# Keys and values from seven block products in four passes, stored once in float

## The chip, the cores and the metric

The kernel runs on one core of one Trainium2 chip. The metric is the device time of one execution in microseconds; three executions of the kernel before took 2989.80, 2990.52 and 2991.84 us, so the median is 2990.52 us.

## The reference, cut to what matters

Two layers follow each other on `x` (8 batches of 256 tokens, width 1024). The change touches only how the second layer gets its keys and values from the context, 2048 rows of width 1024, and how they reach its attention (32 query heads, 8 key heads, 128 wide). In short, for each batch:

```python
k = rope((ctx @ L1_xattn_wk).reshape(256, 8, 128))    # x * cos + concat(-x2, x1) * sin, over the token's angle
v = (ctx @ L1_xattn_wv).reshape(256, 8, 128)
p = softmax(where(mask, q @ k.T / sqrt(128), -1e9))    # query head h uses key head h // 4
x = x + tanh(g_xattn) * (concat_heads(p @ v) @ L1_xattn_wo)
```

All of it is in float32. The kernel gets that precision on TensorE by writing each factor as a high part (its value rounded to float32r) and a low part (what is left), and adding three products: high by high, high by low, low by high.

## The kernel before

The five engines (PE, ACT, DVE, POOL and SP, which issues DMAs) run one written-out program each, in order; they meet only in semaphores. `wait_ge(*at(name, key))` waits until the instruction that was marked with `inc(name, key)` is done. `three` (lines 147 to 152) issues the three products of one piece, each a matmul of 128 rows, a 128x128 stationary part and 512 columns. `weave` (from line 3130) sets the order in which the stages' programs follow each other on each engine; each stage is a generator and each `next` runs it to its next `yield`.

The stages are: keys and values (`kv_tensor`, `kv_scalar`, `kv_vector`, `kv_gpsimd`, `kv_sync`, 0 to 367 us), the first layer's attention by Fourier transforms (`ac_`, from 334 us), the first feed-forward layer (`f0_`), the queries (`qp_`, which already uses seven block products for eight with block sums on POOL), the attention with its output product (`at_`, about 1600 to 2800 us) beside which the last layer's weights are prepared (`wf_`), and the last layer (`f1_`).

Keys and values: 64 outputs of 128x512, each 8 pieces of 128 along the width (`C` = 8) by 3 matmuls. ACT rounds a loaded piece (`kv_high`), DVE or POOL subtracts to get the low part. The split weights stay in SBUF; the context is loaded and split in four blocks of 512 rows (`renew`). An output leaves its PSUM bank so: a value by a copy on ACT (high) and a subtraction on DVE (low); a key is first turned by its angles, by three products on DVE (lines 389 to 391), a sum on POOL (432), a copy on ACT (330) and a subtraction on POOL (434). High and low parts are stored in HBM, `kd[0]`, `kd[1]`, `vd[0]`, `vd[1]`. The last 8 value outputs are laid between the first steps of the `ac_` stage: its tables and its first 256 rows are loaded and split while PE still works on values.

Attention: 128 steps (`u`), four for each pair of a key head and 512 tokens (`n = u // 4`, 32 of them). `load_kv(n)` issues four DMAs for the high and low parts two steps ahead, and nothing else has to be done to them. Each step has on PE the transposes of weights, 12 score matmuls of 256 columns, 6 value matmuls and 24 output matmuls of 512; on DVE the maxima, the weights' scaling (`weigh`), the low parts and the sum into `at_xt`; on ACT the exponentials and copies; on POOL the low parts of the queries (`split_q`) and, in the first quarter, of the output weights (`split_wo`).

## Time and profile before

| | |
|---|---|
| median of three executions | 2990.52 us (2989.80 to 2991.84) |
| the profiled execution, first to last instruction | 2990.3 us |
| PE busy | 2959.3 us, 99% |
| DVE, POOL, ACT busy | 67%, 46%, 43% |
| bytes moved | 488.29 MB, mean 163 GB/s |

The profile gives for each engine the time in which it was busy, for each group of instructions their number, mean duration and the idle time in front of them with its releaser, and for each stretch of time the granted clock of TensorE (1.00 is 2.4 GHz). A matmul's duration is from its issue to its modelled end and overlaps its successor's, so the work rate of PE is read from the distance between starts and not from durations. Span and measured median differ by 0.2 us.

### The profile page before, as it was taken

The page shows a single profiled execution, that of the slowest core. Times are in us where ns is not written, and L with a number is a line of the kernel's source. Part 1 is how long each engine was busy: PE and PEld are TensorE (multiplying, and loading weights), DVE is VectorE, ACT ScalarE, POOL GpSimd, SP SyncE. Part 2 cuts the span into 40 slices and gives each one's busy share as a digit, 9 for nine tenths or more (in the row PEclk, how much of TensorE's full clock was granted, in tenths as well). Part 3 has the DMA queues.
Part 4 walks back from the last instruction along what each step waited for, and adds up shares of the span by engine and source line. Part 5 has one row for each costly group of instructions (what it writes and reads, how often), then busy time and mean ns, then how long its engine had stood idle before and what let it go on. Part 6 is the DMA issues. An engine that isn't in the chain of part 4 may idle for free.

```text
span 2990.3 us, 41114 instructions
## 1 busy us (share of the span) xinstructions
PE 2959.3 (99%) x14701; PEld 2482.3 (83%) x14701; DVE 2009.8 (67%) x4714; ACT 1282.8 (43%) x2686; POOL 1369.9 (46%) x1105
## 2 busy tenths in 40 slices
PE   9999999999999999999999999999999999999999
PEld 7888878887788878887888888888888888888887
DVE  4432478888655686679667777666776676666566
ACT  4111366665422422232223666555555545544332
POOL 2422388886422587777776334322322211111264
PEclk9999999999999999999999999999999999999999
DMA  7332421212555564455444787676677666665531
GB/s 254 127 120 99 166 70 50 78 64 75 191 177 166 197 179 113 113 149 152 109 112 120 242 268 239 227 242 209 193 221 244 189 196 204 208 194 166 225 108 76
DMA packets 320661, 488.29 MB, mean 163 GB/s; under 512 B 26236, under 2 KB 155644, under 8 KB 317644
## 3 DMA queue, kind: packets, MB, share of 16 engines
q1 hardware_dynamic: 319740, 484.23, 51.0%
q8 instruction: 118, 1.93, 0.3%
q10 hardware_dynamic: 720, 1.44, 0.1%
q14 instruction: 83, 0.68, 0.1%
HBM read 324.12 MB, written 161.48 MB: 162 GB/s over the span
## 4 chain that ended last, share of the span: by engine, by line
PE 61%; DVE 3%; DMA 0%; issue 0%; POOL 0%; ACT 0%; SPq 0%; DVEq 0%; ACTq 0%
PE PB L150 19%; PE PB L151 19%; PE PB L152 19%; PE PB L2401 4%; DVE qp_b L2150 1%; PE PB L2830 0%; DVE PB L2192 0%; DMA qp_raw<-in_wq 0%; DVE qp_r L2198 0%; DVE PB L2174 0%; DVE qp_c L2194 0%; DVE qp_r L2188 0%; DVE qp_r L2189 0%; POOL f1x L3046 0%; DMA qp_in<-xod 0%
## 5 line engine op out<-in xcount | busy, mean ns | idle before, releaser
L2567 POOL TENSOR_TENSOR at_ql<-at_qf,at_qh 128x512 fp32r<-128x512 f32 x128 | 166.2, 1299 | 833.9 <-ACT at_qh L2441 833.9
L2448 ACT ACTIVATE at_ss<-at_ss,at_sm,at_bs 128x256 f32<-128x256 f32 x512 | 301.9, 591 | 317.1 <-DVE at_sm L2528 317.1
L150 PE MATMUL PB<-at_woh,at_ah 128*128 128x512 f32 x1024 | 400.4, 391 | 0.6 <-DVE at_al L2550 0.6
L151 PE MATMUL PB<-at_wol,at_ah 128*128 128x512 f32 x1024 | 399.9, 390 | 0.0
L152 PE MATMUL PB<-at_woh,at_al 128*128 128x512 f32 x1024 | 399.5, 390 | 0.0
L2558 DVE SCALAR_TENSOR_TENSOR at_xt<-PB,gt,at_xt 128x512 f32<-128x512 f32 x256 | 192.1, 750 | 249.7 <-PE PB L152 249.5
L150 PE MATMUL PB<-qp_b,qp_a 128*128 128x512 f32 x896 | 350.2, 391 | 8.4 <-DVE qp_r L2196 3.8
L151 PE MATMUL PB<-qp_b,qp_a 128*128 128x512 f32 x896 | 349.3, 390 | 0.0
L152 PE MATMUL PB<-qp_b,qp_a 128*128 128x512 f32 x896 | 349.2, 390 | 0.0
L2220 POOL TENSOR_TENSOR qp_a<-qp_raw,qp_a 128x512 fp32r<-128x512 f32 x192 | 260.0, 1364 | 101.2 <-ACT qp_a L2112 98.5
L2112 ACT ACTIVATE qp_a<-qp_raw 128x512 fp32r<-128x512 f32 x192 | 113.5, 625 | 292.1 <-POOL qp_raw L2224 162.4
L2460 ACT ACTIVATE at_pth<-PB 128x512 fp32r<-128x512 f32 x256 | 139.2, 596 | 225.0 <-PE PB L2401 225.0
L152 PEld LDWEIGHTS PB<-at_woh,at_al 128*128 128x128 f32 x1024 | 192.3, 188 | 41.0
L150 PEld LDWEIGHTS PB<-at_woh,at_ah 128*128 128x128 f32 x1024 | 192.7, 188 | 37.5 <-ACT at_ah L2471 0.8
L151 PEld LDWEIGHTS PB<-at_wol,at_ah 128*128 128x128 f32 x1024 | 192.7, 188 | 35.3
L150 PEld LDWEIGHTS PB<-qp_b,qp_a 128*128 128x128 f32 x896 | 168.5, 188 | 45.9 <-DVE qp_r L2196 4.9
L152 PEld LDWEIGHTS PB<-qp_b,qp_a 128*128 128x128 f32 x896 | 168.6, 188 | 35.5
L151 PEld LDWEIGHTS PB<-qp_b,qp_a 128*128 128x128 f32 x896 | 168.6, 188 | 34.6
L2544 DVE TENSOR_TENSOR at_ptl<-PB,at_pth 128x512 fp32r<-128x512 f32 x256 | 164.8, 686 | 40.5 <-ACT at_pth L2460 40.5
L2524 DVE CUSTOM_DVE_ANT_0 at_ss<-PB,at_bi 128x256 f32<-128x256 f32 x512 | 185.4, 418 | 0.2
L150 PE MATMUL PB<-at_kh,at_qh 128*128 128x256 f32 x512 | 154.8, 302 | 0.0
L2538 DVE TENSOR_SCALAR at_ss<-at_ss,at_sm 128x256 f32<-128x256 f32 x512 | 149.3, 356 | 4.5
(314 smaller groups left out, 7570.6 us busy)
## 6 DMA issues: line engine op xcount, KB each, us to landing
at_woh<-wod SPq DMA_DIRECT2D x48, 1024.0 KB, 7.4
at_wol<-wod SPq DMA_DIRECT2D x48, 1024.0 KB, 9.6
qp_raw<-in_wq SPq DMA_DIRECT2D x32, 1024.0 KB, 5.4
qd<-qp_r SPq DMA_DIRECT2D x256, 128.0 KB, 2.5
at_qf<-qd SPq DMA_DIRECT2D x128, 256.0 KB, 3.4
at_rawo<-in_wo SPq DMA_DIRECT2D x32, 512.0 KB, 5.3
...
```

Source lines behind the costliest of these rows:

```text
L150: pe.matmul(o, ah, bh, start=start, stop=False)
L151: pe.matmul(o, ah, bl, start=False, stop=False)
L152: return pe.matmul(o, al, bh, start=False, stop=stop)
L2220: pool.tensor_tensor(qp_part(pair, i, 1), qp_weight(pair, i), asf(qp_part(pair, i, 0)), ALU.subtract).then_inc(*inc("qp_pool", ("w", pair, ...
L2401: m = pe.transpose(PB[1][:, 512 * k + P * c:512 * k + P * c + P], at_ss[s][:, c, P * k:P * k + P], idt[:, :])
L2448: m = act.activation(at_ss[s][:, c, :], at_ss[s][:, c, :], ACT.Exp, bias=z[:, 4 + c:5 + c], scale=at_bs[:, qn % 2, 8 + 2 * b + c % 2:9 + 2 ...
L2460: self.act.activation(at_pth[:, k, :], BK[2 + k], ACT.Copy).then_inc(*inc("at_act", ("pt", u, k)))
L2524: dve.tensor_tensor_reduce(out=at_ss[s][:, c, :], in0=PB[0][:, L * c:L * c + L], in1=at_bi[qn % 2][:, 2 * b + c % 2, :], scale=1.0, scalar ...
L2538: dve.tensor_scalar(at_ss[s][:, c, :], at_ss[s][:, c, :], z[:, 12 + c:13 + c], None, ALU.mult).then_inc(*inc("at_dve", ("weight", u, c)))
L2544: self.dve.tensor_tensor(at_ptl[:, k, :], BK[2 + k], asf(at_pth[:, k, :]), ALU.subtract).then_inc(*inc("at_dve", ("pt", u, k)))
L2558: self.dve.scalar_tensor_tensor(out=xt, in0=BK[6 + p % 2], scalar=gt[:, 2:3], in1=xt, op0=ALU.mult, op1=ALU.add).then_inc(*inc("at_dve", ( ...
L2567: self.pool.tensor_tensor(at_ql[n % 3][:, :], at_qf[n % 2][:, :], asf(at_qh[n % 3][:, :]), ALU.subtract).then_inc(*inc("at_pool", ("q", n)))
```

## The change

Context and weights are each cut in two by two blocks of 512x512 for a pass; a pass gives 1024 token rows by 1024 columns of keys or of values (`KV_PASSES`: values, keys, keys, values), from seven block products instead of eight, with four block sums on each side and sums of products behind. A product is 4 tiles (output 128x512) by 4 pieces (`c`) by 3 matmuls. Sums S1, S2 and S4 of the context's side are made on POOL, S3 and all sums T1 to T4 of the weights' side on DVE. Every product's 8 factor pieces are rounded on ACT and their low parts made on DVE (side `b`, and piece 3 of side `a`) or POOL (pieces 0 to 2 of side `a`); nothing of them is kept for the next pass. They go through a ring of 10 pieces a side, made 6 pieces ahead in each engine's program. The first three products run piece by piece across the four tiles, the others tile by tile.

Products are added up in SBUF (`leave`): 2 of 7 are copied by ACT, the others added by DVE, with one more sum on POOL. Keys and values are stored once, as plain floats: 64 stores of 256 KB where there were 128. Loads are 8 MB a pass, four times, where context and weights were loaded once (16 MB).

The turn by the angles and the split of keys and values move into attention, once for each `n`: on POOL two products (`turn_k`), and two low parts (`split_k`, `split_v`); on DVE two sums over 64 partitions (`join_k`); on ACT two copies. `load_kv` issues four DMAs as before: keys straight, keys with their halves swapped (two), and values.

The `ac_` stage's first loads wait for the last use of the raw blocks in whose place they go (`kv_spent`), several of its tiles move to other addresses, and its first steps are laid between the last products.

```diff
-        kd = [nc.dram_tensor(f"kd{i}", [G, P, T], F, kind="Internal").ap() for i in range(2)]
+        kd = nc.dram_tensor("kd", [G, P, T], F, kind="Internal").ap()
...
+        KV_SEQ = (0, 4, 3, 1, 6, 2, 5)
+        KV_PASSES = (("v", 0), ("k", 0), ("k", 1), ("v", 1))
+        KV_N = 7 * len(KV_PASSES)
+        KV_RING = 10
...
+        KV_FACTOR = {"a": ("a11", "a11", "a21", "s1", "a12", "a22", "a12"), "b": ("b11", "b11", "b12", "t1", "b21", "b21", "b22")}
+        KV_SUM = {("a", 3): ("kv_pool", "S1"), ("a", 1): ("kv_pool", "S2"), ("a", 2): ("kv_dve", "S3"), ("a", 6): ("kv_pool", "S4"),
+                  ("b", 3): ("kv_dve", "T1"), ("b", 1): ("kv_dve", "T2"), ("b", 2): ("kv_dve", "T3"), ("b", 5): ("kv_dve", "T4")}
...
+        def kv_low(side, c):
+            return "kv_dve" if side == "b" or c == 3 else "kv_pool"
+        def kv_bank(n, t):
+            return 4 + t % 2 if n >= KV_N - 2 else 4 * (n % 2) + t
+        def kv_emptied(n, t):
+            return ("kv_act" if n % 7 in (0, 2) else "kv_dve", ("out", n, t))
...
+        def kv_schedule(do):
+            do.begin()
+            for q in range(6):
+                do.prepare(q // 4, q % 4)
+            for n in range(KV_N):
+                do.product(n)
+                for t in range(4):
+                    if 4 * n + 6 + t < 4 * KV_N:
+                        do.prepare(n + 1 + (2 + t) // 4, (2 + t) % 4)
+                    do.tile(n, t)
+                    do.leave(n, t)
+                    do.load(n, t)
+                    if n >= KV_N - 2 and t % 2 and (n, t) != (KV_N - 1, 3):
+                        yield
+                if KV_N - 5 < n < KV_N - 2:
+                    yield
...
+            def chunk(self, n, t, c):
+                on, ts = self.on, slice(P * t, P * t + P)
+                for side in ("a", "b"):
+                    on.wait_ge(*at("kv_act", (side, n, c)))
+                    on.wait_ge(*at(kv_low(side, c), (side, n, c)))
+                rows, cols = ("a", "b") if KV_PASSES[n // 7][0] == "v" else ("b", "a")
+                m = three(self.pe, BK[kv_bank(n, t)], (kv_part(rows, n, c, 0)[:, ts], kv_part(rows, n, c, 1)[:, ts]),
+                          (kv_part(cols, n, c, 0), kv_part(cols, n, c, 1)), c == 0, c == 3)
+                if c == 3:
+                    m.then_inc(*inc("kv_pe", ("out", n, t)))
+                elif t == 3:
+                    m.then_inc(*inc("kv_pe", ("chunk", n, c)))
+            def product(self, n):
+                if n < 3:
+                    for c in range(4):
+                        for t in range(4):
+                            if c == 0:
+                                self.claim(n, t)
+                            self.chunk(n, t, c)
+            def tile(self, n, t):
+                if n > 2:
+                    self.claim(n, t)
+                    for c in range(4):
+                        self.chunk(n, t, c)
...
+        class KvScalar(Keys):
...
+            def prepare(self, n, c):
+                on, p, i = self.on, n // 7, KV_SEQ[n % 7]
+                for side in ("a", "b"):
+                    if (side, i) in KV_SUM:
+                        engine, what = KV_SUM[side, i]
+                        on.wait_ge(*at(engine, (what, p, c)))
+                        on.wait_ge(*at(*kv_loaded(KV_FACTOR[side][i], p, c)))
+                    if 4 * n + c >= KV_RING:
+                        on.wait_ge(*at(*kv_chunk_done(4 * n + c - KV_RING)))
+                    self.act.activation(kv_part(side, n, c, 0), kv_factor(side, n, c), ACT.Copy).then_inc(*inc("kv_act", (side, n, c)))
...
+        class KvVector(Keys):
...
+            def low(self, side, n, c):
+                self.on.wait_ge(*at("kv_act", (side, n, c)))
+                self.dve.tensor_tensor(kv_part(side, n, c, 1), kv_factor(side, n, c), asf(kv_part(side, n, c, 0)), ALU.subtract).then_inc(
+                    *inc("kv_dve", (side, n, c)))
+            def first_sums(self, p, c):
+                dve, on = self.dve, self.on
+                on.wait_ge(*at(*kv_loaded("b11", p, c)))
+                on.wait_ge(*at(*kv_loaded("b12", p, c)))
...
+                dve.tensor_tensor(kv_raw["t1"][:, c, :], kv_raw["b12"][:, c, :], kv_raw["b11"][:, c, :], ALU.subtract).then_inc(
+                    *inc("kv_dve", ("T1", p, c)))
+                on.wait_ge(*at(*kv_loaded("a11", p, c)))
+                on.wait_ge(*at("kv_pool", ("S1", p, c)))
+                dve.tensor_tensor(kv_raw["a21"][:, c, :], kv_raw["a11"][:, c, :], kv_raw["a21"][:, c, :], ALU.subtract).then_inc(
+                    *inc("kv_dve", ("S3", p, c)))
+            def prepare(self, n, c):
+                dve, on, p, k = self.dve, self.on, n // 7, n % 7
+                if n == 2:
+                    self.first_sums(0, c)
+                self.low("b", n, c)
+                if kv_low("a", c) == "kv_dve":
+                    self.low("a", n, c)
+                if k == 1 and p:
+                    self.first_sums(p, c)
+                b11, b12, b21, b22, t1 = (kv_raw[name][:, c, :] for name in ("b11", "b12", "b21", "b22", "t1"))
+                if k == 2:
+                    on.wait_ge(*at(*kv_loaded("b22", p, c)))
...
+                    dve.tensor_tensor(b11, b22, t1, ALU.subtract).then_inc(*inc("kv_dve", ("T2", p, c)))
+                if k == 3:
+                    dve.tensor_tensor(b12, b22, b12, ALU.subtract).then_inc(*inc("kv_dve", ("T3", p, c)))
+                if k == 4:
...
+                    dve.tensor_tensor(b21, b21, b11, ALU.subtract).then_inc(*inc("kv_dve", ("T4", p, c)))
+            def leave(self, n, t):
+                dve, on, p, k, bank = self.dve, self.on, n // 7, n % 7, BK[kv_bank(n, t)]
+                c11, u, f, st = (a[t][:, :] for a in (kv_c11, kv_u, kv_f, kv_st))
+                if k in (0, 2):
                     return
+                on.wait_ge(*at("kv_pe", ("out", n, t)))
+                if k == 1:
+                    on.wait_ge(*at("kv_act", ("out", n - 1, t)))
...
+                    m = dve.tensor_tensor(st, c11, bank, ALU.add)
+                if k == 3:
...
+                    m = dve.tensor_tensor(u, c11, bank, ALU.add)
+                if k == 4:
+                    on.wait_ge(*at("kv_pool", ("out", n - 1, t)))
...
+                    m = dve.tensor_tensor(st, f, bank, ALU.add)
+                if k == 5:
+                    dve.tensor_tensor(f, f, bank, ALU.add)
+                    m = dve.tensor_tensor(u, u, bank, ALU.add)
+                if k == 6:
+                    on.wait_ge(*at("kv_dve", ("out", n - 1, t)))
+                    m = dve.tensor_tensor(u, u, bank, ALU.add)
+                m.then_inc(*inc("kv_dve", ("out", n, t)))
...
+        class KvGpsimd(Keys):
...
+            def prepare(self, n, c):
+                pool, on, p, k = self.pool, self.on, n // 7, n % 7
+                if n == 2:
+                    self.first_sum(0, c)
+                if kv_low("a", c) == "kv_pool":
+                    on.wait_ge(*at("kv_act", ("a", n, c)))
+                    pool.tensor_tensor(kv_part("a", n, c, 1), kv_factor("a", n, c), asf(kv_part("a", n, c, 0)), ALU.subtract).then_inc(
+                        *inc("kv_pool", ("a", n, c)))
+                if k == 1 and p:
+                    self.first_sum(p, c)
+                a11, a12, s1 = (kv_raw[name][:, c, :] for name in ("a11", "a12", "s1"))
+                if k == 2:
...
+                    on.wait_ge(*at("kv_dve", ("S3", p, c)))
+                    on.wait_ge(*at("kv_pool", ("S1", p, c)))
+                    pool.tensor_tensor(a11, s1, a11, ALU.subtract).then_inc(*inc("kv_pool", ("S2", p, c)))
+                if k == 3:
...
+                    pool.tensor_tensor(a12, a12, a11, ALU.subtract).then_inc(*inc("kv_pool", ("S4", p, c)))
+            def leave(self, n, t):
+                if n % 7 == 3:
+                    on = self.on
+                    on.wait_ge(*at("kv_dve", ("out", n, t)))
+                    on.wait_ge(*at("kv_act", ("out", n - 1, t)))
+                    self.pool.tensor_tensor(kv_f[t][:, :], kv_f[t][:, :], kv_u[t][:, :], ALU.add).then_inc(*inc("kv_pool", ("out", n, t)))
...
+        class KvSync(Keys):
...
+            def begin(self):
+                for c in range(4):
+                    self.fetch("b11", 0, c)
+                for c in range(4):
+                    self.fetch("a12", 0, c)
+                    self.fetch("b21", 0, c)
+                for c in range(4):
+                    self.fetch("b12", 0, c)
+                    self.fetch("a21", 0, c)
+                    self.fetch("a22", 0, c)
+                for c in range(4):
+                    self.fetch("b22", 0, c)
+                self.sp.dma_start(idt[:, :], ident).then_inc(*landed("ident_in", 0))
...
             next(kv)
             next(ac)
-            for beside in (2, 2, 1):
-                next(kv)
-                next(kv)
-                for _ in range(beside):
-                    next(ac)
+            next(kv)
+            next(ac)
+            next(ac)
+            next(kv)
+            next(ac)
+            next(ac)
+            next(kv)
+            next(kv)
+            next(ac)
             for _ in kv:
                 pass
             next(ac)
...
+                if u % 4 == 3 and n < NG:
+                    do.join_k(n)
+                    do.split_k(n)
...
+                if u % 4 == 2 and n < NG:
+                    do.turn_k(n)
...
+            def join_k(self, n):
+                dve, on, kr, ks = self.dve, self.on, at_kr[n % 2], at_ks[n % 2]
+                on.wait_ge(*at("at_pool", ("sine", n)))
+                dve.tensor_tensor(kr[0:64, :, :], kr[0:64, :, :], ks[0:64, :, :], ALU.subtract).then_inc(*inc("at_dve", ("turned", n, 0)))
+                dve.tensor_tensor(kr[64:P, :, :], kr[64:P, :, :], ks[64:P, :, :], ALU.add).then_inc(*inc("at_dve", ("turned", n, 1)))
...
+            def turn_k(self, n):
+                pool, on, kr, ks = self.pool, self.on, at_kr[n % 2], at_ks[n % 2]
+                c, s = (qp_rope[:, k, :, :].rearrange("p t n -> p (t n)").unsqueeze(1).to_broadcast([P, 2, L]) for k in range(2))
+                on.wait_ge(*at("qp_rope", 1))
+                on.wait_ge(*at(f"at_k{n % 2}", ("swapped", n, 1)))
+                pool.tensor_tensor(kr[:, :, :], kr[:, :, :], c, ALU.mult).then_inc(*inc("at_pool", ("cosine", n)))
+                pool.tensor_tensor(ks[:, :, :], ks[:, :, :], s, ALU.mult).then_inc(*inc("at_pool", ("sine", n)))
+            def split_k(self, n):
+                self.on.wait_ge(*at("at_act", ("k", n)))
+                self.pool.tensor_tensor(at_kl[n % 2][:, :], at_kr[n % 2][:, :, :].rearrange("p b n -> p (b n)"), asf(at_kh[n % 2][:, :]),
+                                        ALU.subtract).then_inc(*inc("at_pool", ("k", n)))
+            def split_v(self, n):
+                self.on.wait_ge(*at("at_act", ("v", n)))
+                self.pool.tensor_tensor(at_vl[n % 2][:, :, :], at_vr[n % 2][:, :, :], asf(at_vh[n % 2][:, :, :]), ALU.subtract).then_inc(
+                    *inc("at_pool", ("v", n)))
...
-                sp.dma_start(asf(at_kh[s][:, :]), kd[0][g][:, rows]).then_inc(*landed(f"at_k{s}", ("high", n)))
-                sp.dma_start(asf(at_kl[s][:, :]), kd[1][g][:, rows]).then_inc(*landed(f"at_k{s}", ("low", n)))
-                sp.dma_start(asf(at_vh[s][:, :, :]), vd[0][rows, cols].rearrange("(t p) d -> p t d", p=P)).then_inc(*landed(f"at_v{s}", ("high", n)))
-                sp.dma_start(asf(at_vl[s][:, :, :]), vd[1][rows, cols].rearrange("(t p) d -> p t d", p=P)).then_inc(*landed(f"at_v{s}", ("low", n)))
+                sp.dma_start(at_kr[s][:, :, :].rearrange("p b n -> p (b n)"), kd[g][:, rows]).then_inc(*landed(f"at_k{s}", ("straight", n)))
+                for k in range(2):
+                    sp.dma_start(at_ks[s][64 * k:64 * k + 64, :, :].rearrange("p b n -> p (b n)"), kd[g][64 - 64 * k:P - 64 * k, rows]).then_inc(
+                        *landed(f"at_k{s}", ("swapped", n, k)))
```

## Rows read from the trace of the kernel before

**Rows 1.** The page: busy time, share of the span and instructions of TensorE.
```profile
PE 2959.3 (99%) x14701; PEld 2482.3 (83%) x14701; DVE 2009.8 (67%) x4714; ACT 1282.8 (43%) x2686; POOL 1369.9 (46%) x1105
```

**Rows 2.** Busy time by stretch: us, each engine's busy us (instructions), granted clock, DMA share, GB/s.
```profile
7.00:312.00 305.00, 304.94 (x1344) 252.21 (x1345) 116.68 (x167) 71.22 (x118) 97.38 (x76) 1.00 0.42 146
1600.00:2800.00 1200.00, 1199.10 (x6529) 1033.62 (x6528) 846.22 (x2521) 637.11 (x1613) 323.28 (x228) 1.00 0.66 212
760.00:800.00 40.00, 35.14 (x167) 26.84 (x166) 28.82 (x72) 16.91 (x22) 20.67 (x25) 0.96 0.51 168
1340.00:1400.00 60.00, 54.03 (x229) 43.58 (x228) 57.96 (x68) 15.71 (x28) 47.12 (x32) 0.97 0.51 129
```

**Rows 3.** Waits of PE, 0 to 660 us: total us, times, longest.
```profile
PE PB L659 <- POOL ac_slw L1025: 1.4, 3, 0.6
PE PB L298 <- ACT kv_wvh L350: 1.3, 1, 1.3
```

**Rows 4.** PE in order of time, late in the stage: start us, duration us.
```profile
304.62 0.39 PE L150 MATMUL PB<-kv_ch,kv_wkh 128*128 128x512 f32 x1
...
311.88 0.39 PE L152 MATMUL PB<-kv_ch,kv_wkl 128*128 128x512 f32 x1
```

**Rows 5.** Groups of instructions, 7 to 312 us: busy us, mean ns, idle before.
```profile
L432 POOL TENSOR_TENSOR kv_t<-kv_t,kv_t 128x512 f32<-128x512 f32 x31 | 40.0, 1290 | 101.7 <-DVE kv_t L391 101.7
...
L389 DVE TENSOR_TENSOR kv_t<-PB,kv_rt 128x512 f32<-128x512 f32 x31 | 21.4, 691 | 75.7 <-PE PB L152 68.3 <-POOL kv_ol L434 7.4
...
L330 ACT ACTIVATE kv_oh<-PB 128x512 fp32r<-128x512 f32 x24 | 13.6, 596 | 36.8 <-PE PB L152 31.7 <-DMA vd<-kv_ol 4.9
...
L404 DVE TENSOR_TENSOR kv_wvl<-kv_rc,kv_wvh 128x512 fp32r<-128x512 f32 x16 | 13.2, 853 | 14.0 <-ACT kv_wvh L350 14.0
...
L404 DVE TENSOR_TENSOR kv_wkl<-kv_rc,kv_wkh 128x512 fp32r<-128x512 f32 x16 | 10.9, 693 | 8.3 <-ACT kv_wkh L350 8.2
```

**Rows 6.** DVE and POOL at once, both on SBUF operands, in order of time.
```profile
1384.59 1.65 DVE L2194 TENSOR_TENSOR qp_c<-qp_c,qp_rope 128x512 f32<-128x512 f32 x1
...
1385.77 1.62 POOL L2216 TENSOR_TENSOR qp_raw<-qp_raw 128x512 f32<-128x512 f32 x1
```

**Rows 7.** The first microseconds: ACT and PE by time, then two stretches as in rows 2.
```profile
5.73 0.63 ACT L346 ACTIVATE kv_ch<-kv_rc 128x512 fp32r<-128x512 f32 x1 [1.76 <-DMA kv_rc<-in_ctxT]
...
7.03 2.06 PE L298 MATMUL PB<-kv_wvh,kv_ch 128*128 128x512 f32 x8 [1.30 <-ACT kv_wvh L350]
...
4.00:10.00 6.00, 4.69 (x16) 2.70 (x14) 3.08 (x3) 3.08 (x6) 2.62 (x2) 1.00 0.94 323
50.00:60.00 10.00, 10.00 (x46) 8.29 (x45) 4.74 (x7) 2.40 (x4) 0.81 (x1) 1.00 1.01 356
```

**Rows 8.** The passage to the `ac_` stage in order of time: DVE, POOL, ACT, PE.
```profile
324.55 0.96 DVE L847 TENSOR_TENSOR ac_tl<-ac_tr,ac_th 128x768 fp32r<-128x768 f32 x1
...
328.13 0.21 DVE L859 BATCH_NORM_AGGREGATE ac_st<-ac_st 128x2 f32<-128x12 f32 x1
334.52 1.23 DVE L943 TENSOR_TENSOR ac_ql<-ac_xn,ac_qh 128x1024 fp32r<-128x1024 f32 x1 [6.18 <-ACT ac_qh L710]
...
336.86 2.95 DVE L847 TENSOR_TENSOR ac_tl<-ac_tr,ac_th 128x1024 fp32r<-128x1024 f32 x3
...
330.19 0.24 POOL L983 TENSOR_SCALAR ac_st<-ac_st 128x2 f32<-128x2 f32 x1
...
331.87 1.52 ACT L702 ACTIVATE ac_xn<-ac_xb,ac_st 128x512 f32<-128x512 f32 x2 [4.25 <-POOL ac_st L991]
...
336.58 0.39 PE L150 MATMUL PB<-ac_qh,ac_th 128*128 128x512 f32 x1
```

**Rows 9.** One attention step in order of time: DVE, then PE.
```profile
1910.95 0.75 DVE L2558 SCALAR_TENSOR_TENSOR at_xt<-PB,gt,at_xt 128x512 f32<-128x512 f32 x1 [1.13 <-PE PB L152]
...
1911.83 1.14 DVE L2538 TENSOR_SCALAR at_ss<-at_ss,at_sm 128x256 f32<-128x256 f32 x4
...
1914.84 1.04 PE L2401 MATMUL PB<-idt,at_ss 128*128 128x128 f32 x8
```

509 lines of the change are left out of this document (186 added, 323 removed).

## The prediction

> **What bounds the kernel now.** I read the page first: PE is busy for 2959.3 of 2990.3 us [rows 1], so only what PE does or waits for can move the end. Then the stretches: from 7 to 312 us, where keys and values are made, PE has 304.94 of 305 us of work at the full clock of 2.4 GHz, and DVE 117, POOL 97, ACT 71 us; in the attention PE has 1199.10 of 1200 [rows 2]. The waits of PE say the same: up to 660 us they are single microseconds [rows 3]. So this stage is bound by the number of its matmuls. Their rate is in the order of time: 33 starts, 304.62 to 311.88 us, are 32 distances, 0.2269 us each [rows 4].
>
> **What goes.** Before, 64 outputs x 8 pieces x 3 = 1536 matmuls; after, 28 products x 4 tiles x 4 pieces x 3 = 1344. They have the same shape, so 192 x 0.2269 = **43.6 us** leave PE. A product is 48 matmuls, 10.9 us; a tile 2.72 us; a pass 76.2 us.
> The Trainium skill ("TensorE: Matmul & The Clock Gate", section "Wait — 56ns, not 53.3ns?") gives 215.7 ns between starts at 512 columns; by that the part would be 41.4 us. The row of this kernel decides.
>
> **Side engines, pass for pass.** ACT: 56 roundings at 0.63 [rows 7] and 8 copies at 0.60 [rows 5], 40 us of 76: no bound. POOL: 21 low parts, 12 sums, 4 sums of products, 37 x 1.29 [rows 5] = 48 us. DVE: 28 + 7 low parts and 20 sums, 55 instructions with both inputs in SBUF at 0.69 (the weights' low parts while POOL is idle), and 24 sums with one input in PSUM at 0.69 [rows 5]: 54.5 us. All fit, if they don't disturb each other. They do: where DVE and POOL both work on SBUF, a DVE instruction of this size takes 1.65 and the POOL instruction beside it 1.62 [rows 6], against 0.69 and 1.29 alone. So a POOL instruction can cost DVE 1.65 - 0.69 = 0.96 us. The lower bound is the opening, where 16 low parts on DVE met 8 on POOL and took 853 ns for 693 [rows 5]: 16 x 0.16 / 8 = 0.32. Between them a pass is 54.5 + 37 x 0.32 = 66 us or 54.5 + 37 x 0.96 = 90 us of DVE, beside 76.2 of PE. I take 0.65, between them since here both engines are released by the same ACT copies, 0.63 apart, but DVE is not in demand all the time as in rows 6's stretch (57.96 of 60 us [rows 2]): 78.5 us, though back-to-back instructions overlap by some 0.05 each, which gives 75. It is just covered. The last piece of a product is made from 2.7 us into the product before, and needed 2 us into its own, some 8 us after it can be ready; this takes the bunched sums (positions 7, 1 and 2 of a pass) nearly. I put **3 us** (0 to 30) for waits in passes 2 to 4.
>
> **The start.** Before, the first matmuls can go with high parts alone, at 7.03 us [rows 7]; now a piece waits for all four parts, so for the POOL low part, 1.29 after the ACT copy that ends at 6.36: about 7.8, **0.8 us** later. Data: product 2 needs three blocks, so 7 blocks, 7.3 MB, by its last piece at 37.8 us, and the T2 sums (in DVE's order ahead of the next piece) the eighth. At 323 to 356 GB/s [rows 7] eight blocks are there by about 27 us: loads are hidden, unless the rate falls to the 146 GB/s of the stage [rows 2], where the supply followed demand. The engines are not hidden: for each of product 2's pieces, S1, T1, S3, two low parts, S2 and T2 go through DVE and POOL, about three POOL and four DVE instructions, 5.5 us at the crowded rate, from 20 us (when ACT has copied the first sums) to about 38; then low part and S4 on POOL, low part and T3 on DVE and a sum of products for each of product 3's, 3.2 us. Product 3 is the first by tiles: it wants all four pieces within 2 us of 40.5 us, and gets the last at about 47.9. So **5.4 us**. Bounds: 0.6 with 0.32 for a meeting, 11 if product 2 is late as well. Together 6.2.
>
> **The passage to `ac_`.** Before, 8 outputs (43.5 us) lie beside it, the first two ahead of the tables and statistics; the chain is table low part at 324.55, statistics to 328.34, POOL to 331.8, ACT to 334.5, the queries' low part to 335.75; PE takes it at 336.58 [rows 8]. So it has only 0.8 us of room and is 11.2 us long. Half of it waits for a context split on POOL (its statistics start at 330.19), which now comes earlier: 9.5 us remain. After the change DVE reaches it when product 25 is through, T + 11.9 if T is that product's start, and ends at T + 21.4. PE has only product 25 and half of product 26 before the spectra, 16.3 us, and 2.7 of spectra: it asks at T + 19.0, **2.4 us** early. Then DVE has three low parts and four sums of products (4.5 us) and the second table's low part, 1.2 [rows 8], ahead of the odd spectra: ready at T + 27.1, asked at T + 24.2, **2.9 us**. The correlation behind has 1.6 us of room. What DVE is late by in product 25 comes on top; I put 6.0 in all, 0.5 to 9.
>
> **The clock.** Where PE stood for 4.9 us in 40, and 6 in 60, the mean granted clock was 0.96 and 0.97 [rows 2]: part of the time at 1.2 GHz, 1.6 and 1.8 us lost. Two such places: **1.5 us**, 0 to 3.5.
>
> **Attention.** Per key head and block, 32 times: POOL 4 x 1.29, DVE 2 x 0.69, ACT 2 x 0.62: 165, 44 and 40 us beside 1200 in which POOL has 323, DVE 846 and ACT 637 [rows 2]. DVE's two sums come ahead of `weigh`, in a gap of 1.13 us (1909.82 to 1910.95); they push it by 0.25, and it ends at 1912.97, 1.87 before PE's transposes at 1914.84 [rows 9]. The keys' low part is ready at 1914.2 of such a step, the scores want it at 1915.6. The cover of both is that room; without it each is about 0.3 us x 32. On POOL the wait for the swapped keys has `split_wo` behind it, but the keys were issued seven microseconds before. The moved steps issue four DMAs on SP's queue as before; in the keys' stage SP has half the stores and twice the loads. The first `n` falls into the end of the queries' stage. I put **1 us**, 0 to 4; not below nothing, as no matmul goes there.
>
> **Sum.** 2990.3 - 43.6 + 6.2 + 3 + 6.0 + 1.5 + 1 = 2964.4, and 0.2 to the median: **2964.5**.
>
> **Rivals.**
> A. All of it is hidden: a meeting costs 0.32, so the start costs 1.4 us, the passes nothing, the passage 5: 2990.5 - 43.6 + 6.5 = 2953. For it: the opening's own rows. Against it: the 1.65 of rows 6. From 2948 to 2956.
> B. DVE becomes the stage's bound, and the kernel is slower. Its mechanism is the meeting of two-SBUF-input instructions on DVE with POOL at the full 0.96: 90 us a pass for 76.2, less the 0.05 of overlap for 79 instructions, 86: 10 us x 4 = 40 and, with start 11, passage 9 and clock 3.5, 2990.5 - 43.6 + 63 = 3010. It gives a loss from (43.6 - 17) / 4 = 6.7 us a pass on, so from about 0.87 us per POOL instruction. The clock of a starved PE would add to it. For it: both engines' programs bunch their sums; against it: POOL has no more than half of the time, and a DVE instruction with a PSUM input beside a POOL one took 0.69 [rows 5].
> The Trainium skill ("SBUF — State Buffer", section "Who interferes with whom") has the rule for this: a DVE instruction with two SBUF inputs and a POOL instruction that reads SBUF hold one port in turn, each whole. By it every meeting costs the full POOL instruction, which is B if they always meet. Rows 6 agree with the rule; how often they meet, no row shows.
> C. In between: DVE is late by 2 to 5 us in each pass: 2976 to 2985, by the same rows at 0.75 to 0.8.
> D. The attention is not free: the keys' low part comes late in every fourth step by 1 us, 32 us: 2990.5 - 43.6 + 16.7 + 32 = 2996. The gain would be nearly gone and the kernel slightly slower. For it: 1.4 us of room only; against it: it is POOL's first work in that step and POOL idles there.
> E. The matmuls don't get fewer on the clock, as the new operands' layout slows the stream. The queries' stage does the same products in the same layout, so 2 in 100.
>
> **How the numbers follow.** Forecast with its own range 2956 to 2976: 0.56. A: 0.10. C: 0.17. B: 0.09, of which 0.02 ends within 0.2% of before. D: 0.06, half of it within 0.2%. E: 0.02. The range 2949 to 2984 leaves out B, D and E and the tail of A and C, about 2 in 10. A measurement of this kernel tells 0.2%, 6 us, from no change (2984.5 to 2996.5): faster 0.83, within 0.07, slower 0.10.
>
> **What would show it.** In the changed kernel: 1344 matmuls in the stage and the first `ac_` matmul some 27 us earlier than 333.86; PE waits of about 5 us between 40 and 50 us whose releasers are DVE or POOL low parts; two waits of 2 to 3 us at the first spectra; DVE instructions with two SBUF inputs at a mean near 1.1 us in the stage, near 0.8 for A, near 1.4 for B; DVE busy over 90% of passes 2 to 4; no new waits of PE in attention but a few tenths. The prediction is wrong if the steady passes starve PE, if the 8 MB of the start come slower than 300 GB/s, or if a load at a pass boundary is late, which I take as covered by the ten microseconds between a block's last use and its next.

## The result and the profile after

The changed kernel takes 3031.94 us (median; 3026.1 to 3042.75), the kernel before 2990.66 (2989.8 to 2991.84) beside it: a ratio of 1.014, 95% interval 1.0121 to 1.016. It is some 41 us slower, where 26 us faster was forecast. The profiled execution spans 3030.8 us, against 2990.3.

The page, busy time by engine; it answers to [rows 1]:

```profile
PE 2944.2 (97%) x14509; PEld 2460.7 (81%) x14509; DVE 2268.2 (75%) x4916; ACT 1379.4 (46%) x2878; POOL 1676.8 (55%) x1303
```

The 192 matmuls are gone (14701 - 14509), and yet PE is busy for only 15 us less: slower matmuls count as busy. To see where the time went I read in each trace when PE first takes certain tiles, in us from the start of the span:

```
kernel            ac_qh    at_kh    f1w     span    at_kh to f1w
before            336.6   1617.0   2818.6   2990.3   1201.6
after             331.0   1612.2   2859.1   3030.8   1246.9
e1_straight       328.2   1607.7   2809.1   2980.9   1201.4
e2_turn_last      328.1   1609.4   2845.9   3017.9   1236.5
e12_weigh_only    328.0   1611.3   2841.2   3013.3   1229.9
e9_weigh_early    328.2   1611.5   2820.5   2992.3   1209.0
e6_weigh_act      328.1   1609.5   2876.7   3048.5   1267.2
e7_both           329.9   1608.1   2875.4   3047.4   1267.3
e4_fill           369.3   1659.6   2912.6   3084.7   1253.0
e4b_fill_r        329.7   1611.8   2863.9   3035.8   1252.1
e3_pool_small     301.3   1582.5   2834.9   3006.6   1252.4
e5_no_dve_sums    314.1   1594.8   2841.1   3012.9   1246.3
e10_start_dve     324.8   1609.5   2821.4   2993.5   1211.9
e11_more_dve      318.9   1602.6   2812.9   2984.7   1210.3
e13_two_chunks    318.9   1601.8   2813.2   2984.9   1211.4
e14_last_pass     319.9   1598.9   2809.2   2981.0   1210.3
e15_both_moves    318.4   1595.8   2804.9   2976.6   1209.1
```

`ac_qh` is the first work that needs the whole chain of the passage, so it marks the end of the stage of keys and values; `at_kh` begins attention, `f1w` is the last stage. The mark is not quite the end: in the trace of before 96 matmuls of keys and values lie behind it, after the change 72, so that only 168 of the 192 are gone by then, 38.1 us. From before to after: the stage gains 5.6 us, the middle loses 0.8 although the other 24 lie there, attention loses 45.3, the last stage nothing: 40.5 us in all. The same code reached `ac_qh` between 328.0 and 331.0 us in seven profiles, so differences there count from 3 us on.

Stretches of the changed kernel, as in [rows 2] (us; each engine's busy time and instructions; granted clock; DMA share; GB/s):

```profile
0.00:60.00 60.00, 46.34 (x160) 34.02 (x161) 49.17 (x41) 29.81 (x54) 44.49 (x32) 0.86 0.50 172
45.00:65.00 20.00, 13.86 (x35) 9.86 (x35) 20.00 (x21) 9.55 (x18) 14.56 (x10) 0.60 0.38 120
120.00:196.00 76.00, 73.92 (x325) 60.48 (x324) 72.43 (x78) 33.22 (x62) 58.90 (x37) 1.00 0.52 167
320.00:350.00 30.00, 25.17 (x97) 20.01 (x97) 19.44 (x27) 14.88 (x22) 11.16 (x11) 0.89 0.17 59
1620.00:2000.00 380.00, 355.51 (x1896) 303.92 (x1895) 285.81 (x776) 213.58 (x507) 176.09 (x111) 0.98 0.68 218
```

From 45 to 65 us DVE does not rest for a moment, PE works for 13.9 of 20 us, and its clock is 0.60: mostly the lower of its two levels (1.2 GHz of 2.4). This clock is not the same in every execution: in six other profiles of the same code it is 0.68 (e7) to 0.76. A steady pass (120 to 196 us) has DVE at 95%. In attention it is the first third that falls behind.

Waits of PE in the changed kernel (us in total, times, longest), from 120 to 350 us and then in attention:

```profile
PE PB L150 <- ACT kv_b L318: 5.7, 3, 1.9
PE PB L150 <- DVE ac_ql L954: 2.8, 1, 2.8
PE PB L150 <- ACT ac_kk L741: 2.0, 1, 2.0
...
PE PB L150 <- POOL at_wol L2635: 18.2, 8, 3.5
PE PB L2426 <- DVE at_ss L2580: 14.1, 13, 2.0
PE PB L150 <- POOL at_kl L2622: 2.1, 1, 2.1
```

Attention's waits come to 35.9 us with two small ones, where before it had almost none; the rest of its 45.3 us lies for the most part with matmuls at the lower clock (0.98 over the 380 us above is up to 7.6 us). Two things are late: the low part of the output weights, and the softmax weights `at_ss`, which DVE multiplies by the reciprocal sums in `weigh`. On POOL's own list of waits stands one for a transfer, the swapped rows of the keys:

```profile
POOL at_kr L2617 <- DMA at_ks<-kd: 14.0, 8, 4.1
```

### The profile page after: what moved, and what is told of

It is laid out like the page before. It is cut to its first block, busy times and chain, and to the rows that moved or that the text cites. A ratio compares the mean times of both kernels' runs of the same rounds, so it can differ in the third digit from the quotient of the medians.

```text
span 3030.8 us, 41686 instructions
## 1 busy us (share of the span) xinstructions
PE 2944.2 (97%) x14509; PEld 2460.7 (81%) x14509; DVE 2268.2 (75%) x4916; ACT 1379.4 (46%) x2878; POOL 1676.8 (55%) x1303
## 4 chain that ended last, share of the span: by engine, by line
PE 54%; DVE 5%; DMA 2%; POOL 2%; ACT 1%; issue 0%; SPq 0%; DVEq 0%; POOLq 0%; ACTq 0%
PE PB L150 17%; PE PB L151 17%; PE PB L152 17%; PE PB L2426 3%; DMA at_ks<-kd 2%; DVE at_ss L2580 1%; POOL at_wol L2635 1%; DVE qp_b L2159 1%; DMA qp_raw<-in_wq 0%; PE PB L2892 0%; POOL at_kr L2617 0%; POOL at_ks L2618 0%; DVE PB L2201 0%; DVE qp_r L2207 0%; POOL qp_a L2229 0%
## 5 line engine op out<-in xcount | busy, mean ns | idle before, releaser
L150 PE MATMUL PB<-at_woh,at_ah 128*128 128x512 f32 x1024 | 403.4, 394 | 18.9 <-POOL at_wol L2635 18.2
L2580 DVE TENSOR_SCALAR at_ss<-at_ss,at_sm 128x256 f32<-128x256 f32 x512 | 180.1, 416 | 4.5
```

The source lines that it names most:

```text
L150: pe.matmul(o, ah, bh, start=start, stop=False)
L2580: dve.tensor_scalar(at_ss[s][:, c, :], at_ss[s][:, c, :], z[:, 12 + c:13 + c], None, ALU.mult).then_inc(*inc("at_dve", ("weight", u, c)))
```

## The experiments

**Attention alone.** e1_straight takes the new work out of attention:

```
-                    do.join_k(n)
-                    do.split_k(n)
...
-                    do.turn_k(n)
...
-                    do.split_v(n)
...
+                sp.dma_start(asf(at_kh[s][:, :]), kd[g][:, rows]).then_inc(*landed(f"at_k{s}", ("high", n)))
+                sp.dma_start(asf(at_kl[s][:, :]), kd[g][:, rows]).then_inc(*landed(f"at_k{s}", ("low", n)))
```

> The changed kernel, with attention's new work left out: keys and values go from their float blocks straight into the high and the low tiles, by four transfers of 256 KB as in the kernel before, and nothing is turned, joined or split there (the scores come out wrong, the work of TensorE is the same). Theory: all of attention's loss is the added work on GpSimd and VectorE. Then the stretch from the first score to the first product of the last stage goes from 1246.9 us back to 1202 to 1204, and the time from 3032 to 2987 +-3. Rival: attention is slower for another reason (float blocks, where the stage starts, the clock): the stretch stays over 1230 and the time over 3015.

Measured: 2984.03 us, 0.9976 of before (0.9967 to 0.9986); attention 1201.4 us, as before the change. So the added work is the whole loss of attention, 45 us, and the stage of keys and values alone is worth 7 us of the 43.6.

**Where `turn_k` stands.** POOL in the changed kernel, in a step with turning (start us, duration us, what it waited for):

```profile
1793.21 1.30 POOL L2609 TENSOR_TENSOR at_ql<-at_qf,at_qh 128x512 fp32r<-128x512 f32 x1 [5.32 <-ACT at_qh L2467]
1796.14 1.29 POOL L2617 TENSOR_TENSOR at_kr<-at_kr,qp_rope 128x512 f32<-128x512 f32 x1 [1.63 <-DMA at_ks<-kd]
1797.40 1.26 POOL L2618 TENSOR_TENSOR at_ks<-at_ks,qp_rope 128x512 f32<-128x512 f32 x1
1798.62 2.33 POOL L2635 TENSOR_TENSOR at_wol<-at_rawo,at_woh 128x1024 fp32r<-128x1024 f32 x1
```

The queue stands still for 1.63 us until the swapped rows have landed, then turns for 2.5 us, and only then makes `at_wol`, for which PE waits. e2_turn_last moves the two products behind `split_wo`:

```
-                if u % 4 == 2 and n < NG:
-                    do.turn_k(n)
...
                 do.split_wo(u)
+                if u % 4 == 2 and u // 4 + 1 < NG:
+                    do.turn_k(u // 4 + 1)
```

> The changed kernel, with the two products of turn_k issued at the end of step 4k+2, behind split_wo, and no longer ahead of it. Theory one (the order on GpSimd's queue: turn_k waits for the swapped rows and split_wo waits behind it, and its products lie beside VectorE's weighing): the 18.2 us of TensorE waits for at_wol go, those for at_ss (14.1 us) fall to under 4, the stretch of attention is 1204 to 1215 us and the time 2990 to 3002. Theory two (what counts is that GpSimd's work delays VectorE wherever it lies): at_wol goes, the waits for at_ss stay over 10 us, the time is 3008 to 3018. Rival (the swapped rows are late for any place): new waits for at_kh or at_kl, time over 3015.

Measured: 3019.07 us, 1.0106 (1.0081 to 1.0132); attention 1236.5. The waits for `at_wol` are gone, those for `at_ss` have grown from 14.1 to 20.5 us. The time lies just above the second theory's range. Its mechanism stands in order of time, around one such wait: POOL, DVE, then PE's transposes of `at_ss`:

```profile
1763.46 1.30 POOL L2622 TENSOR_TENSOR at_kl<-at_kr,at_kh 128x512 fp32r<-128x512 f32 x1 [3.11 <-ACT at_kh L2471]
1764.72 1.33 POOL L2609 TENSOR_TENSOR at_ql<-at_qf,at_qh 128x512 fp32r<-128x512 f32 x1
1766.01 1.31 POOL L2627 TENSOR_TENSOR at_vl<-at_vr,at_vh 128x512 fp32r<-128x512 f32 x1
1767.28 2.38 POOL L2635 TENSOR_TENSOR at_wol<-at_rawo,at_woh 128x1024 fp32r<-128x1024 f32 x1
...
1764.03 5.79 DVE L2580 TENSOR_SCALAR at_ss<-at_ss,at_sm 128x256 f32<-128x256 f32 x4
...
1766.26 0.33 PE L2426 MATMUL PB<-idt,at_ss 128*128 128x128 f32 x1 [0.90 <-DVE at_ss L2580]
1767.52 0.33 PE L2426 MATMUL PB<-idt,at_ss 128*128 128x128 f32 x1 [0.94 <-DVE at_ss L2580]
1769.87 1.33 PE L2426 MATMUL PB<-idt,at_ss 128*128 128x128 f32 x5 [2.02 <-DVE at_ss L2580]
```

Four multiplications that took 1.14 us together in [rows 9] take 5.79. They get through one at a time, each where a POOL instruction has ended: PE gets a quarter at 1766.26, 1767.52 and 1769.87, each 0.2 us after POOL's ends at 1766.05, 1767.32 and 1769.66. These instructions have one tensor in SBUF as input, not two. The Trainium skill ("SBUF — State Buffer", section "Who interferes with whom", with "VectorE: DVE Perf Modes", section "Mode 2×_2P — use both read ports for one tensor") says that such a multiplication by a scalar can use both read ports of DVE, and that one of them is GpSimd's too, held for a whole instruction; by that rule it blocks just as a two-input one does, and this trace agrees: the second to the fourth end within 0.16 us of a POOL instruction's end, at 1766.20, 1767.47 and 1769.82.

**`weigh` on another engine.** e6_weigh_act gives the multiplications to ScalarE; e7_both adds e2's move.

```
-                    dve.tensor_scalar(at_ss[s][:, c, :], at_ss[s][:, c, :], z[:, 12 + c:13 + c], None, ALU.mult).then_inc(
...
+                    self.act.activation(at_ss[s][:, c, :], at_ss[s][:, c, :], ACT.Copy, scale=z[:, 12 + c:13 + c]).then_inc(
```

> The changed kernel with the four multiplications by the reciprocal sums (at_ss, 128x256 each, four per step) made by ScalarE (Copy with a scale per partition) and no longer by VectorE; GpSimd's work and order are as they were. Theory (VectorE's multiplications from SBUF to SBUF wait for GpSimd's instructions to end, one for one, and ScalarE's would not): the 14.1 us of TensorE waits for at_ss fall under 2 although ScalarE needs longer for the same tile, the 18.2 us for at_wol stay, attention goes from 1246.9 to 1225 to 1232 us, the time to 3010 to 3017. Rival (the step is simply too full, or ScalarE becomes late): new waits for at_ss, at_pth or at_ah of over 10 us, time over 3025.

> e2_turn_last and e6_weigh_act together: turn_k behind split_wo, and the multiplications on ScalarE. Theory: both kinds of waits of attention are gone and with them the falls of the clock, attention takes 1202 to 1208 us as in the kernel before, and the time is 2986 to 2993, beside e1_straight's 2984. Rival (attention's loss is the sum of the added work): attention over 1220 us, time over 3005.

Measured: 3057.03 us (1.0224, 1.0203 to 1.0244) and 3053.0 us (1.021, 1.0194 to 1.0225); attention 1267 us in both. The waits for `at_ss` did fall to about 2 us, and both expectations were wrong all the same: the rival was right that ScalarE becomes late. In e7's trace, an undisturbed stretch (first ScalarE's four multiplications, then PE's transposes, then those of e2 for comparison):

```profile
2208.72 1.69 ACT L2492 ACTIVATE at_ss<-at_ss,at_sm 128x256 f32<-128x256 f32 x4
...
2200.07 1.66 PE L2426 MATMUL PB<-idt,at_ss 128*128 128x128 f32 x8
2209.84 1.40 PE L2426 MATMUL PB<-idt,at_ss 128*128 128x128 f32 x8
```

```profile
2204.94 1.03 PE L2426 MATMUL PB<-idt,at_ss 128*128 128x128 f32 x8
```

ScalarE reaches them after four exponentials, and finishes at 2210.41 while PE has asked since 2209.84. The eight transposes, 1.03 us in a row, stretch to 1.40 and 1.66, and the list of waits hardly shows that, as each gap is short. Counted from start to start over all 128 steps, the transposes take 26 us more in e6 and 30 in e7 than in the kernel before.

The other half of the loss is in the lists. ScalarE also makes the high part of the output weights, `at_woh`, and is late with that too, so POOL's low part waits for it; in e7, POOL's line and then two of PE's:

```profile
POOL at_wol L2639 <- ACT at_woh L2525: 46.4, 24, 3.6
...
PE PB L150 <- DVE at_sm L2567: 13.8, 8, 1.8
PE PB L150 <- issue: 8.9, 8, 1.1
```

In e2 the first of these is 2.8 us. The list names another engine or none behind PE's 16 waits, but they are waits for output weights: in the order of time each ends 0.10 to 0.26 us after POOL's `at_wol`. They cost 22.7 us in e7 and 29.2 in e6 (18.2 in the changed kernel, nothing in e2).

**`weigh` at another time.** Behind the maxima DVE has a pause, in which POOL is idle too: 1.13 us in a usual step of e2 and not the 1.9 of the expectation, which I read from a step with joins. e9_weigh_early issues `weigh` there, on top of e2; e12_weigh_only does it without e2's move:

```
                 if u < NU:
                     do.scores(u)
+                if 1 <= u < NU + 1:
+                    do.weigh(u - 1)
...
-                if 1 <= u < NU + 1:
-                    do.weigh(u - 1)
```

> e2_turn_last, with VectorE's four multiplications of at_ss issued right behind the score maxima, ahead of the joins, the first half of the output and the rest of the step; nothing is added or left out. In e2's trace VectorE stands idle there for 1.9 us of a usual step, and GpSimd does too, since its split of the queries comes 3.4 us later. Theory (the loss of attention that e2 left is the multiplications' waiting for GpSimd's instructions, one for one): the waits for at_ss fall from 20.5 us to under 2, attention from 1236.5 to 1202 to 1210 us, the time to 2984 to 2994. Rival (the step has too much work, as e6 and e7 could mean): the waits move to at_al, at_ptl or at_kl, attention stays over 1222 us, the time over 3004.

> The changed kernel with the multiplications of at_ss early, as in e9, and turn_k where the change has it, ahead of split_wo. Theory: the 14.1 us of waits for at_ss go, the 18.2 us for at_wol stay, since turn_k waits for the swapped rows with split_wo behind it: attention 1221 to 1230 us, the time 3007 to 3015. Rival (the two kinds of waits are one: what comes late at one place comes late at the other): both fall or neither, attention under 1212 or over 1240 us.

Measured: e9 2994.79 us (1.0014, 1.0004 to 1.0023), attention 1209.0; e12 3015.2 us (1.0083, 1.0068 to 1.0098), attention 1229.9. e9 missed the time's range by a microsecond and met that of attention; e12 met attention's and ended at the edge of the time's. In e12 all waits for `at_ss` are gone and eight of some 2 us for the output weights stay (the list has them as "issue", but each ends 0.10 us after POOL's `at_wol`). The two edits together: 1246.9 to 1209.0, 37.9 us; alone they give 10.4 and 17.0. Each leaves the other's waits standing, and with them some of the fall of the clock (0.97 from 1620 to 2000 us in e2 and in e12, 1.00 in e9). A step of e9, DVE and then POOL:

```profile
1799.76 1.14 DVE L2580 TENSOR_SCALAR at_ss<-at_ss,at_sm 128x256 f32<-128x256 f32 x4
...
1797.21 2.41 POOL L2635 TENSOR_TENSOR at_wol<-at_rawo,at_woh 128x1024 fp32r<-128x1024 f32 x1
1802.73 1.30 POOL L2609 TENSOR_TENSOR at_ql<-at_qf,at_qh 128x512 fp32r<-128x512 f32 x1 [3.12 <-ACT at_qh L2467]
```

The same four multiplications fall into POOL's pause and take 1.14 us again.

**Keys and values: the clock.** Does part of the loss come from the clock that falls after PE's gaps? e4_fill puts 67 matmuls on zeros into the gaps.

```
+                        if (n, c) == (2, 3):
+                            self.fill(BK[7], 14)
...
+                        if (n, t) == (3, 0) and c < 3:
+                            self.fill(BK[7], (10, 9, 16)[c])
...
+                    if (u, i) in ((0, 2), (1, 0)):
...
+                        keep_running(7, (8, 10)[i // 2])
```

> The changed kernel with matmuls on zeros put where TensorE stands idle: 14 ahead of the last chunk of product 2, 10, 9 and 16 ahead of the first three chunks of product 3's first tile, 8 and 10 in the first spectra (67 in all, 15 us at 0.227 us each if TensorE were free for them). Theory (part of the loss is the clock that falls after the gaps, and the gaps themselves are VectorE's): the granted clock from 45 to 65 us goes from about 0.6 to over 0.9 and at 320 to 350 us from 0.89 to over 0.97, the waits take in nearly all the added matmuls, and the time falls by 5 to 10 us to 3022 to 3027. Rival (the clock costs nothing, since VectorE sets the pace in both places): the time stays within 3 us of 3032 or grows by up to 8.

Measured: 3083.22 us (1.0304, 1.0285 to 1.0323). It answers nothing on the clock: the zeros of the 49 fillers at the start were float, not fp32r, and PE waited once for the bank they go to:

```profile
PE PB L275 <- DVE kv_st L406: 13.0, 1, 13.0
```

`ac_qh` came some 40 us late. e4b_fill_r has the zeros in fp32r and takes banks that are empty by then:

```
+        kv_z = place("kv_z", 92, [P, 512], R)
...
+                            self.fill(BK[4], 14)
...
+                            self.fill(BK[5], (10, 9, 16)[c])
```

> The fillers again, in the type of the products (fp32r, 0.227 us each) where the first try had float ones at some 0.88 us: 14 ahead of the last chunk of product 2, 10, 9 and 16 ahead of the first three chunks of product 3's first tile, in banks that have been emptied by then, 8 and 10 in the first spectra. Theory (part of the loss is the clock after the gaps): at 45 to 65 us the granted clock goes from 0.6 to over 0.9, at 320 to 350 us from 0.89 to over 0.97, and the time falls from 3032 to 3022 to 3028. Rival (VectorE sets the pace in both places, the clock costs nothing beside it): the time stays within 3 us of 3032.

Measured: 3029.31 us (1.0123, 1.0106 to 1.0139), `ac_qh` at 329.7. The stretches that answer to those of the change (45 to 65, and 320 to 350 us):

```profile
45.00:65.00 20.00, 16.71 (x68) 13.35 (x68) 20.00 (x20) 10.18 (x20) 15.70 (x10) 0.94 0.30 103
320.00:350.00 30.00, 26.55 (x111) 21.33 (x110) 18.87 (x28) 14.98 (x22) 14.33 (x13) 0.94 0.18 62
```

The clock is back at the start (0.94 for 0.60) and the time is not: the median is 2.6 us lower, with ranges that overlap, and `ac_qh` comes 1.3 us earlier, inside the spread of 3. DVE is busy for all of the 20 us in both kernels. By the time the rival was right, so these fillers are no cure. That the lower clock costs nothing is not shown. From the first product to `ac_qh`, PE's late starts at the lower clock come to 9.4 us after the change and to 5.1 in e4b, its idle time to 21.4 and 12.6, but the 49 fillers take 11.1: they used about half of what the clock gave back. And the five profiles of the same code without fillers that show 0.75 or 0.76 from 45 to 65 us reach `ac_qh` 2.8 to 3.0 us ahead of the one with 0.60, with the same idle time (21.5 to 21.8 us). So the clock may cost some 3 us at the start; no run settles it. In the passage the same code shows 0.89 to 0.94 without fillers, so e4b's 0.94 says nothing there, and it says nothing of attention, where the gaps are short and PE is soon needed again.

**Keys and values: who keeps DVE.** e3_pool_small cuts POOL's instructions to 8 of 512 columns; e5_no_dve_sums cuts DVE's block sums in the same way. One line of each, the first e3's, the second e5's; what each leaves out stands in its expectation.

```
-                    pool.tensor_tensor(a11, s1, a11, ALU.subtract)
+                    pool.tensor_tensor(a11[:, 0:8], s1[:, 0:8], a11[:, 0:8], ALU.subtract)
...
-                    dve.tensor_tensor(b11, b22, t1, ALU.subtract)
+                    dve.tensor_tensor(b11[:, 0:8], b22[:, 0:8], t1[:, 0:8], ALU.subtract)
```

> The changed kernel, where each of GpSimd's instructions in the stage of keys and values covers 8 of its 512 columns (low parts of the context in chunks 0 to 2, S1, S2, S4, the sum into kv_f; TensorE reads the high part where it read that low part, and a22 for s1; the results are wrong). Every semaphore, every instruction of VectorE and its order stay. Theory (VectorE is slow since its two-input instructions on SBUF wait while GpSimd's run): the mean of VectorE's low parts of kv_b falls from 1070 ns to 600 to 650, its share from 95% to under 70%, the idle 13 us of TensorE before 60 us to under 5, the stage gains 22 to 32 us and the time is 3000 to 3010. Rival (VectorE has too many instructions whatever GpSimd does): the means stay over 950 ns, the time over 3025.

> The changed kernel, where VectorE's block sums of keys and values (T1, S3, T2, T3, T4) cover 8 of their 512 columns (b12 is read for t1; results are wrong), GpSimd's work as it was. It asks whether VectorE's demand matters too: 20 of its some 79 instructions of a pass nearly vanish, some 25 us of 72 with their waits for GpSimd. Theory (the loss at the start is VectorE's time including its waits for GpSimd, so either cut brings it back): the idle of TensorE before 60 us falls from 13 to under 6 us, the time to 3003 to 3012, while the mean of the low parts stays over 950 ns. Rival (GpSimd's own pace is the bound at the start): TensorE idle before 60 us stays over 10 us, time over 3022.

Groups of DVE in this stage, from 100 to 320 us, e5's to 300 (busy us, mean ns, idle before). After the change, three; then e3's and e5's:

```profile
L345 DVE TENSOR_TENSOR kv_b<-kv_b,kv_b 128x512 fp32r<-128x512 f32 x66 | 70.6, 1070 | 0.0
L378 DVE TENSOR_TENSOR kv_b<-kv_b,kv_t 128x512 f32<-128x512 f32 x12 | 21.3, 1775 | 0.0
...
L397 DVE TENSOR_TENSOR kv_st<-kv_c,PB 128x512 f32<-128x512 f32 x12 | 8.1, 675 | 0.0
```

```profile
L345 DVE TENSOR_TENSOR kv_b<-kv_b,kv_b 128x512 fp32r<-128x512 f32 x64 | 44.0, 688 | 22.3 <-ACT kv_b L318 22.3
```

```profile
L378 DVE TENSOR_TENSOR kv_b<-kv_b,kv_t 128x8 f32<-128x8 f32 x12 | 15.1, 1255 | 0.0
```

e3: 3003.48 us (1.0045, 1.003 to 1.006), `ac_qh` at 301.3: with POOL quiet DVE's low parts take 688 ns instead of 1070 (600 to 650 were expected), and 27 to 30 us of the stage's loss are gone. DVE's instructions with one input in PSUM took at most 689 ns in the stage of the changed kernel too, beside the busy POOL. e5: 3016.63 us (1.0086, 1.0071 to 1.0101), `ac_qh` at 314.1, half as much. Its time is worse than expected by 5 us, as PE still stood idle for 9.1 of the first 60 us. Its line of the sum T2 is the clearest of all: a sum of 8 columns takes 1255 ns, the length of one POOL instruction. Nearly all of it is waiting.

**A mend.** In the sum of both engines' SBUF work, an instruction is 0.69 us on DVE and 1.25 on POOL. e10_start_dve moves 10 of them to DVE in products 2 and 3 of the first pass, e11_more_dve 17 more in the passes up to the third, e13_two_chunks another 17, e14_last_pass 7 in the last pass, e15_both_moves has all. They stand on e9. This is e10's line, beside which S2 of the first pass moves too; e11 adds `or (c == 2 and 3 < n < 21)`, e13 has `c in (1, 2)` in it, e14 `(c == 2 and n > 3)`.

```
-        def kv_low(side, c):
-            return "kv_dve" if side == "b" or c == 3 else "kv_pool"
+        def kv_low(side, n, c):
+            return "kv_dve" if side == "b" or (c == 3 or n in (2, 3)) else "kv_pool"
```

> e9_weigh_early, and in the stage of keys and values VectorE takes over from GpSimd, for products 2 and 3 of the first pass alone, the low parts of the context in chunks 0 to 2 and S2 (10 instructions of 128x512). Theory (at the start the two engines' instructions on SBUF exclude each other, and the sum of both is what TensorE waits for; VectorE's takes 0.69 us where GpSimd's takes 1.25): 10 instructions shorter by 0.56 us each, so TensorE's idle before 60 us falls from 13 to 5 to 8 us, with some of the clock, and the first matmul on ac_qh comes 6 to 12 us ahead of e9's. Rival (VectorE is the bound by its own count of instructions): VectorE gets 7 us more to do, ac_qh comes 3 to 8 us later.

> e10_start_dve, and from product 4 to the end of the third pass VectorE also makes the context's low part in chunk 2, so 17 of GpSimd's instructions less. Theory (mutual exclusion): VectorE's busy share stays about 95% since it gets 0.69 us of work and loses up to 1.25 us of waiting each time, and the one wait of some 1.9 us per pass boundary shrinks: ac_qh comes 0 to 6 us ahead of e10's. Rival (VectorE's own demand): it comes 3 to 12 us later.

> e11_more_dve, with chunk 1 given to VectorE as well from product 4 to the end of the third pass (so chunks 1, 2 and 3): 17 more of GpSimd's instructions move. Theory (the two engines exclude each other, the sum of both counts): a moved instruction is worth up to 0.6 us as long as VectorE has any waits for GpSimd left to shed, so ac_qh comes 2 to 6 us ahead of e11's 318.9. Rival (VectorE is at its own bound by now, 61 instructions of 0.69 us on SBUF and 24 on PSUM in 75 us): it comes 2 to 10 us later, the time is 2989 to 2997.

> e11_more_dve, with chunk 2's low part on VectorE in the last pass too (7 instructions more). There the turn to the next stage follows, in which VectorE and ScalarE have its first tables and queries to make. Theory (exclusion counts there too): the last product's parts come sooner and ac_qh comes 0 to 3 us ahead of 318.9; the time is 2983 to 2987. Rival (in the turn VectorE's own queue is what is late): ac_qh comes 1 to 4 us later.

> e13_two_chunks and e14_last_pass together. Theory: the gains of both add, since they lie in different passes (the waits of 0.9 us at two pass boundaries in e13, the last product and its passage in e14): 2979 to 2983 us, 0.9960 to 0.9975 of the kernel before. Rival (VectorE's queue carries over into the last pass, so that one of them takes what the other gave): 2983 to 2988.

Measured, each against the kernel before: e10 2991.76 us (0.9998, 0.9989 to 1.0008); e11 2986.87 (0.999, 0.9981 to 1.0); e13 2983.53 (0.9973, 0.9964 to 0.9982); e14 2983.13 (0.9977, 0.9967 to 0.9988); e15 2978.05 (0.9964, 0.9952 to 0.9977). DVE gets more instructions each time, and the kernel gets faster: its demand alone was not the bound. e10 brings `ac_qh` 3.4 us forward, less than expected and hardly beyond the 3 us of spread, though PE's busy time before 60 us grew from 45.38 to 49.19; e11 a further 5.9. e13 and e14 left `ac_qh` where it was, neither what the theory nor what the rival said: e13 takes away the waits at two pass boundaries and finds longer ones in the passage (2.9 and 3.4 us for e11's 2.1 and 1.8). Their medians are 3 to 4 us below e11's, but they were measured apart from it, on another chip, and the ranges overlap. e15 is 1 us better than expected, and clearly faster than both kernels. Its stretch of the steady passes:

```profile
120.00:300.00 180.00, 179.13 (x791) 147.84 (x790) 179.00 (x217) 84.15 (x155) 107.25 (x60) 1.00 0.46 158
```

PE now has all but 0.9 us of 180, so there is next to nothing left to gain there.

## Why the prediction was wrong

Of the 67 us between 2964.5 and 3031.9, 44 lie in attention and 22 ahead of it: by `at_kh` the kernel was to be 26.9 us ahead and was 4.8.

*The 43.6 us.* Right: 192 matmuls left, and in e3, with POOL quiet, `ac_qh` came 35.3 us earlier than before the change (336.6 - 301.3), where 38.1 is all that the matmuls gone by then are worth.

*Attention, the term of 1 us: the step that failed.* It had two errors. "They push it by 0.25, and it ends at 1912.97" took `weigh` with its length of 1.14 us beside an idle POOL, and only meant to add DVE's own two sums (1912.97 is even its end without them; with them it is 1913.22). But the change gives POOL four more instructions per key head, and each of the four multiplications can wait for one of them: 5.79 us in the step above. e9 and e12, which move `weigh` away from them, bring its waits to nothing. I had counted only instructions with two SBUF inputs as ones that meet, and the trace of before could have warned me: its longest `weigh` is 1392 ns, of a median of 349, and I did not ask for it. And "the keys were issued seven microseconds before" took the landing as certain; POOL waited for the swapped rows eight times, 14.0 us, and `split_wo`, which I named as queued behind, was what PE then waited for: 18.2 us. Rival D had the place (a low part late on POOL) but the wrong tile: `at_kl` cost one wait of 2.1 us.

*Side engines.* The duration was right, the consequence was not. I put 75 us of DVE per pass; it is 72.4 of 76, and the mean of the low parts 1070 ns where I said near 1.1 us. (72.4 - 54.5) / 37 is 0.48 us for each POOL instruction. A mean below the pass did not cover it, as the sums are bunched: one wait of 1.9 us in each of passes 2 to 4, 5.7 us, and 0.2 between, for a term of 3.

*The start, 6.2 us.* The place and the releasers were right, the size was not. The first matmul of a product came at 8.72 us, where I had 7.8. Of the waits before 60 us, 13.7 us against the 1.3 of [rows 3], two (start us, duration us, idle before):

```profile
44.62 0.77 PE L150 MATMUL PB<-kv_b,kv_a 128*128 128x512 f32 x1 [4.07 <-DVE kv_a L345]
...
59.78 0.77 PE L150 MATMUL PB<-kv_b,kv_a 128*128 128x512 f32 x1 [3.36 <-issue]
```

The first is product 2's last piece, which I had at about 38 us, the second product 3's first tile, whose last piece I had at 47.9. So product 2's pieces were 7 us later than my 5.5 us for each made them, and from there to product 3's last it took 15 us, where I had 10.

*The passage, 6.0 us.* Two waits of 2.8 and 2.0 us for the two tiles that I named, 2.4 and 2.9 forecast: right (2.1 and 3.4 in e9's profile, where this code is the same).

*The clock, 1.5 us.* By `at_kh` the kernel had gained 4.8 us; 43.6 less the added waits (12.4 at the start, 6.0 in the passes, 4.8 in the passage) would be 20.4. Most of the missing 15.6 us are matmuls at the lower clock, after the gaps: ahead of `ac_qh` 51 of them start 0.30 to 0.57 us after the one before with no idle time in between, where 0.227 is usual, 9.4 us in all, and from there to 400 us it is 3.7 more. As a sum is made this was the largest error in this stage. How much of it is a cost of its own is open: part of it would have been waiting for DVE, which is busy for 20 of 20 us there, and e4b's fillers took half of what they gave back. In attention clock and waits went together (e9), and no run parts them.

*Rivals.* B, DVE bound by its meetings with POOL, was the mechanism, at half of its price per meeting and in attention as well, where I had not looked for it. The range left out this outcome.
